# A reciprocal step divided anew between VectorE, GpSimd and ScalarE, in a token mixer with a routed expert layer

## The reference, cut to what matters

```
x_prev = x shifted by one in time
k, v, r = (mix of x and x_prev) @ Wk.T + bk, ... Wv ..., ... Wr ...        # 4 x 1024 tokens, H = 512
wkv     = scan over time:  out = (e1 * aa + e2 * v) / (e1 * bb + e2)
x       = layernorm(x + (sigmoid(r) * wkv) @ Wo.T + bo)
logits  = x @ wg;  idx = argmax;  gate = softmax(logits)[idx]               # 8 experts
x       = layernorm(x + gate * (x @ W[idx].T + b[idx]))
```

## Time and profile before

| | |
|---|---|
| median of 3 runs | 618.22 us (618.04 to 618.87) |
| the profiled execution | 613.21 us, its span 611.4 us |
| TensorE (PE) busy | 567.8 us, 93% |
| weight loads (PEld) busy | 406.4 us, 66% |
| VectorE (DVE) busy | 536.6 us, 88% |
| ScalarE (ACT) busy | 421.8 us, 69% |
| GpSimd (POOL) busy | 281.0 us, 46% |
| granted TensorE clock | 0.974 of full |

### The profile page before, as it was taken

How to read it: one execution, slowest core, us unless ns; L and a number is a source line. 1 busy time by engine, 2 the same in 40 slices (tenths; PEclk the granted TensorE clock), 3 DMA queues, 4 the chain that set the end, 5 groups by cost and what they waited for, 6 DMA issues and landing times. The chain is left out here.

```text
span 611.4 us, 8910 instructions
## 1 busy us (share of the span) xinstructions
PE 567.8 (93%) x2404; PEld 406.4 (66%) x2405; DVE 536.6 (88%) x854; ACT 421.8 (69%) x799; POOL 281.0 (46%) x221
## 2 busy tenths in 40 slices
PE   3994979999999999999999999999998999999991
PEld 1442556676678668767776876785567878788880
DVE  6898999998999999899899989899999789777770
ACT  3627546596687768658766775956975877788872
POOL 2757634455461454545255344521041465666631
PEclk9998899999999999999999999999987999999996
DMA  9452550075029108404710930667754786877740
GB/s 328 155 65 73 207 69 1 1 214 114 18 85 214 47 1 235 108 0 172 137 34 15 242 88 1 207 142 271 244 163 135 195 237 208 262 231 225 224 154 0
DMA packets 40979, 84.40 MB, mean 138 GB/s; under 512 B 8751, under 2 KB 8751, under 8 KB 40818
## 3 DMA queue, kind: packets, MB, share of 16 engines
q1 hardware_dynamic: 30482, 56.67, 28.0%
q0 software_dynamic: 10464, 27.33, 20.2%
HBM read 66.95 MB, written 35.65 MB: 168 GB/s over the span
## 5 line engine op out<-in xcount | busy, mean ns | idle before, releaser
L1124 POOL TENSOR_TENSOR mixed<-unsplit,mixed 128x1024 fp32r<-128x1024 f32 x42 | 99.6, 2391 | 123.2 <-ACT mixed L775 123.2
L705 PE MATMUL y_ps<-w_e_hi,xgT 128*128 x312 | 109.1, 410 | 0.4 <-issue 0.3
L539 PE MATMUL y_ps<-w_o,rw 128*128 128x512 f32 x224 | 100.8, 594 | 0.0
L526 PE MATMUL vb<-mixed,w_kvr 128*128 128x512 f32 x336 | 85.9, 404 | 3.3 <-DVE evn L1320 3.1
L526 PE MATMUL rb<-mixed,w_kvr 128*128 128x512 f32 x336 | 86.8, 407 | 0.9 <-DVE ee L1334 0.9
L526 PE MATMUL kb<-mixed,w_kvr 128*128 128x512 f32 x336 | 82.8, 395 | 2.6 <-DVE state L1288 2.5
L1140 POOL TENSOR_TENSOR ee<-ee,state 128x512 f32<-128x512 f32 x32 | 36.3, 1135 | 86.6 <-DVE state L1304 85.9
L526 PEld LDWEIGHTS vb<-mixed,w_kvr 128*128 128x128 f32 x336 | 61.9, 188 | 20.9 <-DVE evn L1320 5.4
L526 PEld LDWEIGHTS rb<-mixed,w_kvr 128*128 128x128 f32 x336 | 62.5, 188 | 19.6 <-issue 5.7
L526 PEld LDWEIGHTS kb<-mixed,w_kvr 128*128 128x128 f32 x336 | 62.2, 188 | 18.1 <-DVE state L1288 5.0
L1271 DVE SCALAR_TENSOR_TENSOR unsplit<-diff,vec,xb 128x512 f32<-128x512 f32 x96 | 65.9, 747 | 6.1 <-PE kb L526 5.0
(11 more groups left out here) (234 smaller groups left out, 1094.4 us busy)
## 6 DMA issues: line engine op xcount, KB each, us to landing
bias<-b_experts SPq DMA_DIRECT2D x39, 256.0 KB, 4.5
x_biased<-bo POOLq DMA_DIRECT2D x8, 1024.0 KB, 17.5
w_e_raw<-w_experts SPq DMA_DIRECT2D x8, 1024.0 KB, 8.1
rows<-x_biased SPq DMA_DIRECT2D x28, 256.0 KB, 3.6
x_rows<-rows SPq DMA_DIRECT2D x28, 256.0 KB, 6.7
xb<-xT SPq DMA_DIRECT2D x4, 1026.0 KB, 5.3
xb<-xT SPq DMA_DIRECT2D x3, 1024.0 KB, 5.2
w_raw<-w_square SPq DMA_DIRECT2D x2, 1024.0 KB, 10.9
```

The source lines that it names most:

```text
L526: mm = pe.matmul(bank, w_kvr[m][:, a, h, o:o + P], mixed[m][:, bb, h, :], start=(k == 0), stop=(k == 3 * CH - 1))
L539: mm = pe.matmul(y_ps[:, j % 2, :], rw[:, half, c, j * P:(j + 1) * P], w_o[:, c, :], start=(c == 0), stop=(c == CH - 1))
L705: mm = pe.matmul(y_ps[:, n % 2, :], xgT[n % 3][:, a, c, :], w[:, bass.ds(p, 1), c, :].rearrange("p u o -> p (u o)"), start=(c == 0 and (a, ...
L1124: pool.tensor_tensor(mixed[m][:, LO, 2 * hp:2 * hp + 2, :], unsplit[m][:, LO, 2 * hp:2 * hp + 2, :], mixed[m][:, HI, 2 * hp:2 * hp + 2, :] ...
```

## The change

VectorE loses the middle product: `refine` is gone, and its factor moves into the other two. GpSimd multiplies the numerator of a pair with the first guess (`scale_guess`, 128 x 1024), and VectorE ends with `rw = (2 - ee * er) * (evn * er)`. The new GpSimd product stands ahead of `leave(i, 2)` for pair 0 and ahead of `leave(i + 1, 0)` for pair 1. `result` waits for it. ScalarE waits for the result, no longer for `refine`, before it reuses `ee`.

The means of the first normalisation and both kinds of shifts move from VectorE to ScalarE, as Copy with a factor. Only the two averages of block 6 stay on VectorE.

```
 try_guess(i, p):
-    dve.tensor_tensor(ee[:, p], ee[:, p], er[:, p], ALU.mult)            -> guess_tried
+    dve.scalar_tensor_tensor(ee[:, p] = ee[:, p] * -1.0 * er[:, p])      -> guess_tried
-refine(i, p): er[:, p] = (ee[:, p] - 2.0) * er[:, p]                     -> newton
 result(i, half, p):
+    dve.wait_ge(guess_scaled, g + 1)
-    rw[...] = evn[:, p] * -1.0 * er[:, p]                                -> wkv_done
+    rw[...] = (ee[:, p] + 2.0) * evn[:, p]                               -> wkv_done
+scale_guess(i, p):                                        # on GpSimd, new
+    pool.wait_ge(num_added, i * CH + (2 * p + 2))
+    pool.wait_ge(recip_guess, g + 1)
+    pool.tensor_tensor(evn[:, p], evn[:, p], er[:, p], ALU.mult)         -> guess_scaled
 weight_arg(i, c):                                         # on ScalarE
-    act.wait_ge(newton, (i - 1) * 2 + (p + 1))
+    act.wait_ge(wkv_done, (i - 1) * 2 + (p + 1))
 deviation(n, h):                                          # on ScalarE
+    act.wait_ge(y_taken, n * TPB + (2 * h + 4))
+    act.activation(mean[:, two], row_sum[:, two], ACT.Copy, scale=-1.0 / H)
...
+    act.activation(nmr[...], mean[...], ACT.Copy, scale=rstd[...])       # two of them
 norm2(k, n):                                              # on ScalarE
+    act.activation(nmr2[...], mean2[...], ACT.Copy, scale=rstd2[...])
 step(s) of GpSimd:
     mix_lo(i, R, 0); mix_lo(i, R, 1)
+    scale_guess(i - 1, 1)
     leave(i, 0); add_out_bias(i, ...); leave(i, 1)
     mix_lo(i + 1, K, 0); mix_lo(i + 1, K, 1)
+    scale_guess(i, 0)
     leave(i, 2)
 block 7 of GpSimd: leave(last, 1)
+    scale_guess(last, 0)
     leave(last, 2); leave(last, 3)
+    scale_guess(last, 1)
 step(s) of VectorE: - refine, - average(m, 0), - average(m, 1), - shift(m2, 1), - shift(m, 0)
 expert tiles of VectorE: - shift2(k, n)
```

More of the change, by code:

```diff
@@ L849, in deviation @@
                 two = slice(2 * h, 2 * h + 2)
+                act.wait_ge(y_taken, n * TPB + (2 * h + 4))
+                act.activation(mean[:, two], row_sum[:, two], ACT.Copy, scale=-1.0 / H).then_inc(stats_done, 2)
+                wait(act, logits_done, n * TPB)
                 act.wait_ge(stats_done, n * TPB + (2 * h + 2))
-                wait(act, logits_done, n * TPB)
                 for j in range(2 * h, 2 * h + 2):
@@ L859, in deviation @@
                 act.activation(rstd[:, two], rstd[:, two], ACT.Exp, scale=-0.5).then_inc(rstd_ready, 1)
+                act.wait_ge(rstd_ready, n * 2 + (h + 1))
+                act.activation(nmr[:, 2 * h:2 * h + 1], mean[:, 2 * h:2 * h + 1], ACT.Copy, scale=rstd[:, 2 * h:2 * h + 1])
+                act.activation(nmr[:, 2 * h + 1:2 * h + 2], mean[:, 2 * h + 1:2 * h + 2], ACT.Copy,
+                               scale=rstd[:, 2 * h + 1:2 * h + 2]).then_inc(nmr_ready, 1)
             def norm(n, h):
@@ L1084, in norm2 @@
                 act.activation(rstd2[:, n:n + 1], rstd2[:, n:n + 1], ACT.Exp, scale=-0.5).then_inc(rstd2_ready, 1)
+                act.wait_ge(rstd2_ready, k + 1)
+                act.activation(nmr2[:, n:n + 1], mean2[:, n:n + 1], ACT.Copy, scale=rstd2[:, n:n + 1]).then_inc(nmr2_ready, 1)
                 act.wait_ge(nmr2_ready, k + 1)
@@ L1207, in _ @@
             last = BLOCKS - 1
+            before = last - 1
             mix_lo(last, R, 0)
             mix_lo(last, R, 1)
+            scale_guess(before, 1)
             leave(last, 0)
             add_out_bias(last, BATCH - 1, 1)
-            for c in range(1, CH):
-                leave(last, c)
+            leave(last, 1)
+            scale_guess(last, 0)
+            leave(last, 2)
+            leave(last, 3)
+            scale_guess(last, 1)
             def gather(k):
@@ L1340, in try_guess, with result @@
                 dve.wait_ge(recip_guess, g + 1)
-                dve.tensor_tensor(ee[:, p], ee[:, p], er[:, p], ALU.mult).then_inc(guess_tried, 1)
-            def refine(i, p):
+                dve.scalar_tensor_tensor(out=ee[:, p], in0=ee[:, p], scalar=-1.0, in1=er[:, p],
+                                         op0=ALU.mult, op1=ALU.mult).then_inc(guess_tried, 1)
+            def result(i, half, p):
                 g = i * 2 + p
                 dve.wait_ge(guess_tried, g + 1)
[L1347 to L1353, removed]
+                dve.wait_ge(guess_scaled, g + 1)
                 if not isinstance(i, int) or i > 1:
                     dve.wait_ge(y_filled, (i - 1) * TPB)
-                dve.wait_ge(num_added, i * CH + (2 * p + 2))
-                dve.scalar_tensor_tensor(out=rw[:, half, 2 * p:2 * p + 2, :], in0=evn[:, p], scalar=-1.0,
-                                         in1=er[:, p], op0=ALU.mult, op1=ALU.mult).then_inc(wkv_done, 1)
+                dve.scalar_tensor_tensor(out=rw[:, half, 2 * p:2 * p + 2, :], in0=ee[:, p], scalar=2.0,
+                                         in1=evn[:, p], op0=ALU.add, op1=ALU.mult).then_inc(wkv_done, 1)
             def add_rows(n, j):
@@ L1370, in average @@
                 dve.tensor_tensor(mean[:, two], row_sum[:, two], share[:], ALU.mult).then_inc(stats_done, 2)
[L1372 to L1375, removed]
             def add_two(n, h):
@@ L1601, in _ @@
             recurrence(last, 0)
-            shift(earlier, 1)
             running_max(last, 1)
@@ L1625, in _ @@
             try_guess(last, 0)
-            refine(last, 0)
             result(last, 1, 0)
@@ L1640, in _ @@
             try_guess(last, 1)
-            refine(last, 1)
             result(last, 1, 1)
```

21 lines of the change are left out of this document (5 added, 16 removed).

## The result

The changed kernel takes 622.51 us (median of 5 runs, 621.88 to 623.68) against 618.22 for the kernel before (median of 5, 616.60 to 619.24). The medians are 4.3 us apart. The ratio is 1.0052, 95% interval 1.0030 to 1.0074, which is 3.2 us slower. Forecast were 621.8 us and 617.8 to 625.8. From here on "by the ratio" means the ratio times the time of the kernel before; that and the distance of the medians differ by up to about 1 us in these runs (2 us in e12).

What follows compares the result with a forecast made beforehand. TensorE was taken to bound blocks 3 to 6 and the experts, VectorE block 0 and block 7 with the sorting. Terms 1.3 + 0.2 + 1.0 + 1.0 + 0.1 = +3.6 us on 618.22 gave 621.8 us, range 617.8 to 625.8.

Steps and rivals of the forecast that it cites:

- Rival A: The forecast itself: VectorE and GpSimd take turns, the GpSimd product costs 2.35 us; 621.8 us in all, chance 0.55.
- C: Rival: the GpSimd product doesn't exclude VectorE's products, so the kernel gets faster, 613.1 us; chance 0.12.
- B: Rival: steady blocks pay too, 0.2 to 0.8 us in each of blocks 2 to 6, about 624.5 us; chance 0.15.
- D: Rival: little moves, as block 1's means reach TensorE (-2.3) or the sorting has slack (-2); 619.5 us, chance 0.18.
- +1.5 ahead of block 7: Pair 0 of block 0 at +1.3 us; pair 1 of block 0 and pair 0 of block 1 together +0.2.
- +2.0 from there to the first expert matmul: Both pairs of block 7, +1.0 us each, passed on whole because VectorE has no idle time until the experts.
- only VectorE instructions with both operands in SBUF are concerned: Step on turn-taking with GpSimd: other VectorE instructions are not held, drawn from a 1.27 us scan with a PSUM operand.
- All of it on the path to R3: Pair 0 of block 0: the mix starts 1.3 us later, delaying TensorE's R3 and all that follows.
- the bound of -2.3 us: Averages and shifts in block 1: taken as 0, but -2.3 us if the gain isn't absorbed.
- hidden by TensorE for 38 tiles: Expert stage: a VectorE hop (158 ns) becomes a ScalarE Copy (295 ns), costing only +0.1 us on the last tile.
- The distance between execution and median: The median stood 5.0 us above the profiled execution of 613.21 us; nothing in the change should alter this.

Runs made afterwards that it cites:

- e12: The changed kernel with GpSimd's product of numerator and guess made twice in a row: 647.73 us, ratio 1.0550 to the kernel before.
- e5: The changed kernel, unchanged, timed and traced again on the second chip: 624.37 us, ratio 1.0072 to the kernel before.
- e3: The changed kernel with all averages and shifts back on VectorE, GpSimd product kept in all pairs: 617.71 us, ratio 1.0089 to the kernel before.
- e2: The kernel before with averages and shifts of both normalisations moved to ScalarE, the three VectorE products kept: 611.66 us, ratio 0.9981.
- e4: The changed kernel with both pairs of block 7 in the old three-product form: 612.06 us, ratio 0.9988 to the kernel before.
- e8: The changed kernel with GpSimd's product cut to one element, followed by two constant fills that read nothing: 617.66 us, ratio 0.9949 to the kernel before.
- e6: The changed kernel with only pair 0 of block 0 in the old form: 624.04 us, ratio 1.0060 to the kernel before.
- e7: The changed kernel with the second normalisation's shift back on VectorE: 626.43 us, ratio 1.0093 to the kernel before.
- e11: The same kernel as e10, but with the second normalisation's shift back on VectorE: 612.82 us, ratio 1.0009 to the kernel before.
- e10: The kernel of e2 run again on the third chip: 611.37 us, ratio 0.9985 to the kernel before.

## Why the prediction was right, and where it was not

**The time, +3.6 us: right.** Measured +3.2 us by the ratio (4.3 by the medians); +4.5 in e5 (3.4); +3.94 at the first expert matmul. Rival A holds as a mechanism: turns, and a product of 2.40 us (forecast 2.35). C falls with every pair of the trace. (The chances do not follow from their own weights: A, B and half of D make slower 0.79, and 0.75 was given.) B falls for this kernel with 52.24 us from V1 to V1, although the case it needs, a sum ahead of `try_guess` in pair 1, did occur (390.86): 1.88 us of waiting for ScalarE stood behind it. Without the averages on ScalarE it holds a little (e3), and with a second product fully (e12).

**But the terms were not.** Forecast +1.5 ahead of block 7 and +2.0 from there to the first expert matmul; measured -0.66 and +4.6. By kind of change it is the same: the products were put at +3.5 and cost 5.5 by the ratio (e3; 4.8 by the medians), averages and shifts were put at +0.1 and gave 1.2 (e2). Two errors with opposite signs made the sum, and that it came within half a microsecond is luck.

**Block 7 was undersized.** The step that failed is "only VectorE instructions with both operands in SBUF are concerned". It was drawn from one kind of instruction that was not held, a scan with an operand in PSUM. The trace of before had no small `tensor_scalar` beside a GpSimd sum, but it had a `cast` with one operand:

```profile
425.86 0.28 DVE L1578 CAST counts_i<-counts 128x18 int32<-128x18 f32 x1
```

It ends at 426.14, just as GpSimd's sum on `evn` does (424.83 + 1.27 = 426.10), and takes 0.17 us in the trace after, where GpSimd stands still beside it. This 0.1 us was the sign that was there to see.

Of the 4.6 us from V1 of block 7 on, 0.3 lie ahead of the sorting (V1 to the first sorting step is 16.54 us, in e4 too, against 16.26), so they are not the products'. 2.16 lie at pair 0 instead of 1.0, 1.2 are R3 at the lower clock, which the sum had no term for, and 1.0 is pair 1, as forecast. e4 shows that this block is the loss; e8 that the small instruction is held by GpSimd's writes. That its hold loses the turn to the sum is read from the starts and ends; no run took out this hold alone. The lower clock does not follow from the length of the stop: R3 took 4.61, 4.48, 4.32 and 4.53 us after stops of 3.04 or 3.05 us (changed kernel, e5, e6, e7), 4.40 after 1.79 (e8), but 3.06 after 3.04 in e3.

**Block 0 was oversized.** "All of it on the path to R3" is right (+1.04 in the trace, 1.28 in e6), "and all that follows" is not: 0.66 us is left at block 7, and 0.3 us, within the interval, of the time.

**Averages and shifts were put at 0, and took back what the head cost.** For the first normalisation the bound of -2.3 us that the prediction named, and gave to rival D, was partly true: TensorE's waits of 0.6 and 1.2 us in block 2 go (e2), and V1 of block 7 comes 1.1 us earlier beside the old products, 1.9 us earlier beside the new (389.20 in e5, 391.05 in e3, on different chips). Only with this is the change at -0.66 there. Of the gain 0.4 to 0.55 us reaches the first expert matmul (e2, e11), and none can be told in the time (e11, 1.0009). For the second shift the sum had +0.1, priced at the last tile alone, and there it is right: on the last tile, from the start of ScalarE's last step for `rstd` to the start of the output, it is 0.56 us in e10 and 0.43 in e11. The whole measured -1.5 (e10 against e11, intervals apart); e5 against e7 points the same way, -2.1 by the medians and -1.3 by the ratios, but not clear of noise. The step that failed is "hidden by TensorE for 38 tiles", which left no room for a gain. What stands in its place is open: in e7 TensorE waits 4.5 us for VectorE's `yo` and in e5 0.9, but on the third chip no such wait is listed, and half of the 1.5 us lies outside the recorded span.

**The distance between execution and median** was to stay at 5.0 us. It went to 0. The record does not name the chips of the first runs; what fits is that the profiled execution of before fell on a quick chip and its median came from a slower one. All traces of the first and third chip, and the first one of before (613.21 us), have 132.3 to 134.6 us of experts, whatever the kernel; all of the second chip, and the first one of the change, have 139.8 to 143.7. That the change has no part in it is shown by e7, which has the old expert stage and 143.7 us, and by the four kernels with the new one on quick chips, with 133.1 to 133.4.

**Open:** why 0.7 of the 1.2 us that e10 and e11 have at the start of block 7 are lost inside it (V1 to the first expert matmul is 74.0 us in e2, e10 and e11 against 73.3), and in e11 the rest behind it; how the second shift saves its 1.5 us where TensorE shows no wait; and why the same stop lowers the clock in the changed kernel and not in e3.

**The best version** is e2, run again as e10: the three products stay on VectorE, averages and shifts go to ScalarE. Ratios 0.9981 and 0.9985, about 1 us below before, and 4 to 5 us below the change by the ratios.

## What to carry to other kernels

Before work moves to GpSimd, list everything that VectorE executes in the moved work's time, the eight-element `tensor_scalar` too, and not only the instructions of the same size: where VectorE has no idle time, even the hold of an eight-element instruction moves the queue, and may cost the next turn as well. Look for the one block where the moved work meets other work (here the sorting beside block 7): two pairs of sixteen made nearly the whole loss, and the average block showed nothing. Compare terms and not only sums, and compare only times of one chip.

## What was not expected of the hardware

- A VectorE `tensor_scalar` on 128x8 took 2.35 us beside a GpSimd product of 2.40 us, and 1.09 us beside two fills of 0.52 us, without a turn between them; alone 0.16. A product with two operands in SBUF took 1.16 us beside the same fills.
- After a stop of 3.04 us twelve matmuls took 4.61 us (changed kernel) and 4.48 us (e5), but 3.06 us in e3; after 1.79 us 4.40 (e8); after a stop of 0.93 us, 4.41 us once (e12, granted clock 0.66) and 3.01 us in e4.
- Three chips gave the same kernel 612.9, 621.0 and 612.3 us. On the slower one the time lay in the expert stage with its gathers (139.8 us and more against 134.6 and less), while V1 to V1 kept its 52.2 to 52.4 us.
